# A chunked delta rule on one core: output transposes in four banks, projection in two, and squares, closing norm and output scaling at other slots

## The chip, the cores and the metric

The kernel runs on one core of a Trainium2 chip. The metric is the device time of one execution in microseconds (us). The engines are named as in the profile: PE is TensorE's matmuls and PEld its weight loads, DVE is VectorE, ACT is ScalarE, POOL is GpSimd, and SP (in the timeline SPq) issues most DMAs.

## The reference

The program is four layers over 16 sequences of 512 tokens of 256 channels: a gated linear attention, a mixture of experts, a gated delta rule, and a feed-forward with composed weights. The change touches only the third, whose reference is, cut to its core:

```python
h = _rmsnorm(_layernorm(x, ln1_g, ln1_b), rms_in_w)
q = _causal_conv_silu(h @ Wq, conv_q_w).reshape(b, t, H, Kd)      # H 4, Kd 64, Vd 128
k = _causal_conv_silu(h @ Wk, conv_k_w).reshape(b, t, H, Kd)
v = _causal_conv_silu(h @ Wv, conv_v_w).reshape(b, t, H, Vd)
q = _l2norm(q) * Kd ** (-0.5)
k = _l2norm(k)
g = -jnp.exp(A_log) * jax.nn.softplus(h @ Wa + dt_bias)
beta = jax.nn.sigmoid(h @ Wb)
...
def step(S, inp):
    q_t, k_t, v_t, g_t, b_t = inp
    S = S * jnp.exp(g_t)[..., None, None]
    delta = (v_t - jnp.einsum('bhk,bhkv->bhv', k_t, S)) * b_t[..., None]
    S = S + k_t[..., :, None] * delta[..., None, :]
    return (S, jnp.einsum('bhk,bhkv->bhv', q_t, S))
...
o = _rmsnorm(o, o_norm_w) * jax.nn.silu(h @ Wg)
x = x + o @ Wo
x_out = jax.nn.gelu(_layernorm(x, ln2_g, ln2_b) @ W2 + b2, approximate=False) + x
```

A plain layer norm over the channels follows each layer. The one after the delta rule is the closing norm here. All is float32.

## The kernel before

`delta_rule` takes one sequence a period. A sequence is four chunks of 128 tokens (`TT` = 4), worked in two pairs. The periods are a pipeline: in period b the recurrence of sequence b runs (`here`), while sequence b+1 is projected and convolved (`front`), b+2 is mixed from the experts and normed (`ln`), b-1 gets its last two chunks, its gate, its output projection and the dense layer (`past`), and b-2 its GELU and closing norm (`end`). There are periods -2 to 17. Periods 2 to 13 stand in a hardware loop, two to a turn; period 14 still has all but `ln`.

A period has 16 slots. Each engine has its own `period` function, which writes out the order of its work slot by slot. Nothing is scheduled at run time: each engine works through its queue in that order and waits on semaphores, one for each kind of result. So the order of the lines inside a slot is the order on the engine. A name in `wait("og", 1)` is the semaphore `s["og"]`, here "o is scaled".

For each pair the path is this. `key_products` (TensorE, slots 0 and 8) fills four banks with key by key and key by query products. `products` (VectorE) multiplies them by the decay into `nAT` and `QD`. `send_blocks` (SP) sends the 16 by 16 diagonal blocks of `nAT` to DRAM and reads them back block by block, `invert_blocks` (POOL) inverts them, and `return_blocks` (SP) puts them into `T`. Three levels double the inverted blocks (slots 5 to 7 for pair 0, 13 to 15 for pair 1). In each, `first_half` (TensorE) turns `T` into bank `UT` and multiplies `nAT` into a bank of `YZ`, `half_level` (ScalarE) copies both to `U` and `Y`, `second_half` (TensorE) multiplies them, and `merge` (VectorE) puts the result into `T`; the last level gives `Uf`. Bank `UT` is one for both chunks, so the second chunk's transposes wait for the first one's copy of `U`. The next key products wait for `Uf`.

`chunk` has three parts: `ks` and `R` (part 0), the deltas `dl` and their copy `de` (part 1), the state `S` and the output `o` (part 2). Its slots are in `CHUNK_AT`. Chunk 0 has slots 9 to 11, chunk 1 slots 12 to 14, chunks 2 and 3 slots 0 to 5 of the next period.

The outputs of sequence b-1 go this way: `squares` and `lengths_o`, the power -0.5 on POOL (`orr`), `gated` (the product with the gate), `unit_o` (16 scalings of 128 by 128 on ScalarE), `turn_o` (TensorE, 4 transposes for each of 4 column groups), `turned_o` (the copy to `y`), `mix_out` (the output projection in halves), `residual`, `norm3`, `turn_n`, `dense`. Before the change `turn_o`, `mix_out`, `turn_n`, `dense` and `gate` all use one bank, `SIDE`. `tap` is ScalarE's first term of the convolution, `conv` VectorE's other three, `conv_silu` the silu, `to_tokens` the turn back, `spread_out` its copy.

## Time and profile before

| what | value |
|---|---|
| median of 3 runs | 4717.77 us (4705.86 to 4723.58) |
| profiled execution, own time | 4709.05 us |
| its span | 4707.4 us |
| mean granted TensorE clock | 0.907 of 2.4 GHz |
| PE busy over the span | 4038.7 us (86%) |
| DVE, ACT, POOL busy | 2471.9, 1984.9, 1055.9 us |

The profile page gives the busy time of each engine over the whole program. The delta rule fills the part from about 2100 to 4236 us; what stands in it is read from the timeline, the waits and the table by stretches. A busy time says nothing about who waits for whom; an idle time in brackets in the timeline does, with the engine and line that ended it. The granted clock is 1.0 at 2.4 GHz and 0.5 at 1.2 GHz.

### The profile page before, as it was taken

The numbers are of one execution on the slowest core, as the hardware profiler recorded it, in microseconds if no ns is written. First come the engines' busy times: TensorE is split into PE (matmuls) and PEld (weight loads), VectorE is DVE, ScalarE is ACT, GpSimd is POOL, SyncE is SP. The second block draws the span as 40 slices with busy tenths as digits, with TensorE's granted clock in tenths as the row PEclk, the third lists the DMA queues.
The fourth block names the chain that finished last, engine by engine and source line by source line (L and its number), as shares of the span: only waits on it lengthen the run. The fifth ranks groups of instructions, "written<-read, shape, count | busy, mean of one in ns | idle before, by whom it ended". The sixth has DMA issues, their size and how long they took to land. (4 is left out here: it accounts for less than half of the span.)

```text
span 4707.4 us, 72598 instructions
## 1 busy us (share of the span) xinstructions
PE 4038.7 (86%) x23892; PEld 3132.2 (67%) x23892; DVE 2471.9 (53%) x5457; ACT 1984.9 (42%) x4069; POOL 1055.9 (22%) x1689
## 2 busy tenths in 40 slices
PE   5887887689999999966888888888888888859998
PEld 3555555368888888854666667666666666646666
DVE  7888887432222222225666676766666766421111
ACT  5656564112112211214565565555555555422222
POOL 0111111101221122123333333333333332200000
PEclk8888888899999999987899898888898988879999
DMA  1100100344555555541111111111111110011111
GB/s 33 37 32 27 41 28 28 102 139 171 179 181 189 185 179 181 190 131 52 37 37 37 42 37 41 41 41 32 40 33 37 41 40 21 22 37 58 58 57 46
DMA packets 220431, 345.98 MB, mean 73 GB/s; under 512 B 99956, under 2 KB 171380, under 8 KB 201972
## 3 DMA queue, kind: packets, MB, share of 16 engines
q1 hardware_dynamic: 196404, 271.69, 18.2%
q0 software_dynamic: 23760, 71.07, 4.8%
q8 instruction: 126, 2.06, 0.2%
q14 instruction: 141, 1.16, 0.1%
HBM read 275.56 MB, written 67.63 MB: 73 GB/s over the span
## 5 line engine op out<-in xcount | busy, mean ns | idle before, releaser
L539 ACT ACTIVATE moe_rel<-moe_fc 128x512 f32<-128x512 f32 x284 | 169.6, 597 | 798.7 <-PE moe_fc L504 798.7
L504 PE MATMUL moe_fc<-moe_xT,moe_win 128*128 128x256 f32 x2272 | 504.0, 380 | 1.5 <-issue 0.8
L515 PE MATMUL moe_o<-moe_wout,moe_hT 128*128 128x256 f32 x2272 | 502.0, 379 | 0.0
L504 PEld LDWEIGHTS moe_fc<-moe_xT,moe_win 128*128 128x128 f32 x2272 | 432.9, 191 | 61.2 <-issue 2.1
L515 PEld LDWEIGHTS moe_o<-moe_wout,moe_hT 128*128 128x128 f32 x2272 | 426.3, 190 | 55.1
L563 DVE TENSOR_TENSOR moe_hT<-moe_rel 128x512 f32<-128x512 f32 x284 | 196.6, 692 | 366.5 <-ACT moe_rel L539 366.5
L1781 DVE SCALAR_TENSOR_TENSOR gdr_y<-gdr_bank,gdr_cw,gdr_y 128x511 f32<-128x511 f32 (+2 forms) x384 | 287.5, 749 | 52.6 <-ACT gdr_y L2045 29.0
L2242 PE MATMUL gdr_bank<-gdr_hT,gdr_wqkv 128*128 128x512 f32 x512 | 282.5, 680 | 21.3 <-ACT gdr_qk L2060 15.8
L572 DVE COPY moe_osb<-moe_o 128x512 f32<-128x512 f32 x71 | 49.1, 692 | 424.9 <-PE moe_o L515 424.9
L2361 PE MATMUL gdr_bank<-gdr_ident,gdr_T 128*128 128x128 f32 x768 | 132.5, 301 | 126.5 <-DMA gdr_T<-blocks_in 76.0
L693 PE MATMUL ffn_fc<-ffn_xT,ffn_win 128*128 128x512 f32 x512 | 224.0, 596 | 2.0 <-DMA ffn_win<-ffn_w 2.0
L704 PE MATMUL ffn_o<-ffn_wout,ffn_hT 128*128 128x256 f32 x1024 | 225.2, 381 | 0.0
L737 DVE TENSOR_TENSOR ffn_z<-ffn_o,ffn_xres 128x512 f32<-128x512 f32 x32 | 20.6, 686 | 384.3 <-PE ffn_o L704 384.3
L2365 PE MATMUL gdr_bank<-gdr_T,gdr_nAT 128*128 128x64 f32 x1536 | 215.6, 289 | 0.0
L718 ACT ACTIVATE ffn_hT<-ffn_fc 128x512 f32<-128x512 f32 x128 | 76.4, 597 | 328.2 <-PE ffn_fc L693 328.2
L2361 PEld LDWEIGHTS gdr_bank<-gdr_ident,gdr_T 128*128 128x128 f32 x768 | 102.6, 157 | 166.8 <-issue 74.6
L704 PEld LDWEIGHTS ffn_o<-ffn_wout,ffn_hT 128*128 128x128 f32 x1024 | 193.2, 190 | 27.6
L2365 PEld LDWEIGHTS gdr_bank<-gdr_T,gdr_nAT 128*128 128x128 f32 x1536 | 211.6, 213 | 0.0
L1673 POOL TENSOR_TENSOR gdr_rstd<-gdr_var,gdr_mhalf 128x4 f32<-128x4 f32 x64 | 65.1, 1017 | 648.7 <-DVE gdr_var L91 500.7
L2142 ACT COPY gdr_U<-gdr_bank 128x512 f32<-128x512 f32 x192 | 112.4, 585 | 215.2 <-PE gdr_bank L2361 206.1
L2242 PEld LDWEIGHTS gdr_bank<-gdr_hT,gdr_wqkv 128*128 128x128 f32 x512 | 100.3, 212 | 138.3 <-issue 84.0
L693 PEld LDWEIGHTS ffn_fc<-ffn_xT,ffn_win 128*128 128x128 f32 x512 | 97.8, 191 | 118.9 <-issue 118.2
(394 smaller groups left out, 8591.8 us busy)
## 6 DMA issues: line engine op xcount, KB each, us to landing
moe_win<-in_moe_w SPq DMA_DIRECT2D x71, 1024.0 KB, 8.0
moe_wout<-in_moe_w SPq DMA_DIRECT2D x71, 1024.0 KB, 5.1
slots_out<-moe_osb POOLq DMA_DIRECT2D x71, 256.0 KB, 7.4
ffn_xin<-mixed_rows SPq DMA_DIRECT2D x17, 512.0 KB, 3.8
gla_xp<-in_xT_rows SPq DMA_DIRECT2D x16, 512.0 KB, 4.7
gla_xres<-in_x_rows SPq DMA_DIRECT2D x16, 512.0 KB, 3.9
token_rows<-gla_x POOLq DMA_DIRECT2D x16, 512.0 KB, 3.4
rt_W<-in_fc_b SPq DMA_DIRECT2D x32, 256.0 KB, 3.3
```

What stands on the lines that cost most here:

```text
L504: ins = nc.tensor.matmul(fc_ps[j][:, m % 2, :], win[u][:, c, m * P:(m + 1) * P], xT[:, c, :], start=(c == 0), stop=(c == DT - 1))
L515: ins = nc.tensor.matmul(o_ps[u][:, t, :], hT[u][:, k, t * P:(t + 1) * P], wout[u][:, k, :], start=(k == 0), stop=(k == FT - 1))
L539: nc.scalar.activation(rel[:, j, :, :], fc_ps[j][:], ACT.Relu).then_inc(relu_done, 1)
L563: nc.vector.tensor_tensor(hT[u][:, 2 * j:2 * j + 2, :], rel[:, j, :, :], rel[:, j, :, :], ALU.mult).then_inc(h_ready, 1)
L693: ins = nc.tensor.matmul(fc_ps[m % 4][:], win[:, c, m * P:(m + 1) * P], xT[:, c, :], start=(c == 0), stop=(c == DT - 1))
L704: ins = nc.tensor.matmul(o_ps[t // 2][:, t % 2, :], hT[:, k, t * P:(t + 1) * P], wout[:, k, :], start=(k == 0), stop=(k == FT - 1))
L718: nc.scalar.activation(hT[:, m, :], fc_ps[m % 4][:], ACT.Gelu_apprx_tanh).then_inc(h_ready, 1)
L1781: ins = stt(y[:, n % 4, d:L], bank[FRONT[n % 2]][:, 0:L - d], cw[:, n, 3 - d:4 - d], y[:, n % 4, d:L], ALU.mult, ALU.add)
L2142: done("U", n, copy(U[t][:], heads(bank[UT][:])))
L2242: ins = mm(bank[FRONT[n % 2]][:], wqkv[:, c, n * P:(n + 1) * P], hT[:, c, :], start=(c == 0), stop=(c == DT - 1))
L2361: ins = tp(bank[UT][:, h * P:(h + 1) * P], T[:, i, h, :], ident[:])
L2365: ins = mm(bank[YZ[i]][:, h * HP:(h + 1) * HP].rearrange("p (m n) -> p m n", n=half), nAT[:, i, h, :], first, start=True, stop=True)
```

## The change

`turn_o` writes each of its four column groups to a bank of its own (0, 1, 2, 3) and waits only for that group's scaling; `unit_o` scales one group at a call. `mix_out` uses bank 3 for its first half and bank 0 for its second, and both wait only for the four copies. `products` makes both chunks' `nAT` first, marked by a new semaphore `na` on which SP's send waits, and both `QD` after. The other lines are moves between slots: `squares(3)` and `squares_qk` from slot 5 to 6 on ScalarE, the closing norm's sum and scaling on VectorE from slots 9 and 10 to 2 and 4 and its power on POOL ahead of the others, the key lengths from slot 6 to 7, `unit_o` from slot 8 to 7 and 8, the four turned groups and copies to slot 9, the projection to 10 and 11, and rates, residuals and `norm2` around them. The diff, its lines cut to those that the text speaks of, indentation reduced:

```diff
+TURN_O, MIX = (UT, YZ[0], YZ[1], SIDE), (SIDE, UT)
...
     def send_blocks(pair, b):
-        sp.wait_ge(s["qd"], b * TT + 2 * pair + 2)
+        sp.wait_ge(s["na"], b * TT + 2 * pair + 2)
...
+        if end:
+            power(b - 2, var[1][:], rstd[1][:], "tl_var", 2, "tl_rstd", TT)
...
     def products(pair, b):
         wait, done = waiter(dve, b)
-        for t in (2 * pair, 2 * pair + 1):
-            i = t % 2
-            wait("kk", t + 1)
+        made = lambda i, k: bank[KKB[i][k]][:].rearrange("p (w n j) -> p w n j", w=2, n=H2)
+        for i in range(2):
+            wait("kk", 2 * pair + i + 1)
             for k in range(2):
-                made = bank[KKB[i][k]][:].rearrange("p (w n j) -> p w n j", w=2, n=H2)
-                stt(nAT[:, i, k::2, :], made[:, 0, :, :], -1.0, DT_[i][:, k::2, :], ALU.mult, ALU.mult)
-                ins = tt(QD[t][:, k::2, :], made[:, 1, :, :], DT_[i][:, k::2, :], ALU.mult)
+                ins = stt(nAT[:, i, k::2, :], made(i, k)[:, 0, :, :], -1.0, DT_[i][:, k::2, :], ALU.mult, ALU.mult)
+            done("na", 2 * pair + i + 1, ins)
+        for i in range(2):
+            t = 2 * pair + i
+            for k in range(2):
+                ins = tt(QD[t][:, k::2, :], made(i, k)[:, 1, :, :], DT_[i][:, k::2, :], ALU.mult)
             done("qd", t + 1, ins)
...
-            if slot == 6 and past:
-                lengths_o(b - 1)
...
+            if slot == 2 and end:
+                last_sum(b - 2)
             if slot == 3 and ln:
                 mix(0, b + 2)
             if slot == 4 and past:
                 gated(0, b - 1)
             if slot == 4 and ln:
                 mix(1, b + 2)
+            if slot == 4 and end:
+                last_norm(b - 2)
...
+                lengths_o(b - 1)
                 gated(1, b - 1)
-            if slot == 6 and front:
+            if slot == 7 and front:
                 lengths(b + 1)
-            if slot == 9 and end:
-                last_sum(b - 2)
-            if slot == 10 and end:
-                last_norm(b - 2)
             if slot == 9 and front:
+                rates(0, b + 1)
                 unit(b + 1)
             if slot == 10 and front:
-                rates(0, b + 1)
-            if slot == 10 and ln:
-                norm2(b + 2)
-            if slot == 11 and front:
                 rates(1, b + 1)
                 keys_beta(b + 1)
+            if slot == 10 and past:
+                residual(0, b - 1)
             if slot == 11 and past:
-                residual(0, b - 1)
-            if slot == 12 and past:
                 residual(1, b - 1)
-            if slot == 12 and ln:
-                rms(0, b + 2)
+            if slot == 11 and ln:
+                norm2(b + 2)
             if slot == 13 and past:
                 norm3(b - 1)
             if slot == 13 and front:
                 decay(b + 1, w)
                 values_beta(0, b + 1, w)
+            if slot == 13 and ln:
+                rms(0, b + 2)
...
-    def unit_o(b):
+    def unit_o(h, b):
         wait, done = waiter(act, b)
         act.wait_ge(gate_step, b * 2 + 2)
         wait("orr", 1)
-        for h in range(DH):
-            for t in range(TT):
-                part = o[:, t, h * VD:(h + 1) * VD]
-                ins = a_op(part, part, ACT.Copy, scale=orr[:, t * DH + h:t * DH + h + 1])
-        done("og", 1, ins)
+        for t in range(TT):
+            part = o[:, t, h * VD:(h + 1) * VD]
+            ins = a_op(part, part, ACT.Copy, scale=orr[:, t * DH + h:t * DH + h + 1])
+        done("og", h + 1, ins)
...
-            if past and slot in (10, 11):
-                turned_o(2 * slot - 19, b - 1)
...
+            if past and slot == 9:
+                turned_o(0, b - 1)
+                turned_o(1, b - 1)
             if front and 2 <= slot <= NP_ + 1:
                 spread_out(slot - 2, b + 1)
+            if past and slot == 9:
+                turned_o(2, b - 1)
+                turned_o(3, b - 1)
+            if past and slot == 8:
+                unit_o(2, b - 1)
+                unit_o(3, b - 1)
             if past and 1 <= slot <= TT:
                 gate(slot - 1, b - 1)
             if front and 1 <= slot <= NP_:
                 conv_silu(slot - 1, b + 1)
             if slot == 0 and end:
                 gelu(b - 2)
+            if past and slot == 6:
+                squares(3, b - 1)
+            if front and slot == 6:
+                squares_qk(b + 1)
+            if past and slot == 7:
+                unit_o(0, b - 1)
             if front and slot < NP_:
                 tap(slot, b + 1)
-            if past and slot in (9, 10):
-                turned_o(2 * slot - 18, b - 1)
-            if past and slot in (3, 5):
-                squares(2 if slot == 3 else 3, b - 1)
+            if past and slot == 7:
+                unit_o(1, b - 1)
+            if past and slot == 3:
+                squares(2, b - 1)
             if here and slot in (12, 15):
                 squares(0 if slot == 12 else 1, b)
-            if front and slot == 10:
+            if front and slot == 9:
                 rates(0, b + 1, w)
             if here and slot in (1, 2):
                 decay_keys(slot - 1, b)
-            if past and slot == 8:
-                unit_o(b - 1)
-            if here and slot in (9, 11):
-                decay_keys(2 if slot == 9 else 3, b)
-            if front and slot == 5:
-                squares_qk(b + 1)
-            if ln and slot == 11:
-                lengths_u(b + 2)
+            if here and slot == 11:
+                decay_keys(2, b)
+                decay_keys(3, b)
             if front and slot == 12:
                 rates(1, b + 1, w)
                 channels(0, b + 1, w)
             if front and slot == 13:
                 channels(1, b + 1, w)
                 keep_keys(b + 1)
+            if ln and slot == 12:
+                lengths_u(b + 2)
...
     def turn_o(c, b):
         wait, _ = waiter(pe, b)
-        wait("oTe", c) if c else wait("og", 1)
+        wait("og", c + 1)
         for t in range(TT):
-            ins = tp(bank[SIDE][:, tokens(t)], o[:, t, c * P:(c + 1) * P], ident[:])
+            ins = tp(bank[TURN_O[c]][:, tokens(t)], o[:, t, c * P:(c + 1) * P], ident[:])
         mark("oT", ins)
 
     def mix_out(p, b):
         wait, _ = waiter(pe, b)
-        wait("xe", 1) if p else wait("oTe", DH)
+        wait("oTe", DH)
         for t in (2 * p, 2 * p + 1):
             for c in range(DH):
-                ins = mm(bank[SIDE][:, (t % 2) * D:(t % 2 + 1) * D], y[:, c, tokens(t)], wo_s[:, c, :],
+                ins = mm(bank[MIX[p]][:, (t % 2) * D:(t % 2 + 1) * D], y[:, c, tokens(t)], wo_s[:, c, :],
                          start=(c == 0), stop=(c == DH - 1))
         mark("en", ins)
...
+            if past and slot == 10:
+                mix_out(0, b - 1)
             if here and lv >= BASE:
+                if slot == 13 and past:
+                    pe.wait_ge(s["xe"], b * 2)
                 first_half(lv, 2 * pair, b)
-            if past and slot in (10, 11):
-                turn_o(2 * slot - 19, b - 1)
...
+            if front and slot == 9:
+                rates(b + 1)
+            if past and slot == 9:
+                if here:
+                    pe.wait_ge(s["qd"], b * TT + TT)
+                turn_o(0, b - 1)
+                turn_o(1, b - 1)
             if front and 2 <= slot <= NP_ + 1:
                 to_tokens(slot - 2, b + 1)
             if here and lv >= BASE:
                 gate(slot - 1, b - 1)
             if front and slot < NP_:
                 project(slot, b + 1)
-            if front and slot == 9:
-                rates(b + 1)
-            if past and slot in (9, 10):
-                if slot == 9 and here:
-                    pe.wait_ge(s["qd"], b * TT + TT)
-                turn_o(2 * slot - 18, b - 1)
-            if past and slot in (11, 12):
-                mix_out(slot - 11, b - 1)
+            if past and slot == 9:
+                turn_o(2, b - 1)
+                turn_o(3, b - 1)
+            if past and slot == 11:
+                mix_out(1, b - 1)
```

How this moves ScalarE's queue around the squares, in slots 5 and 6 of a steady period (`gdr_bank0` is `UT`, `gdr_sq<-gdr_qk` the squares of q and k, `gdr_scr,gdr_ov<-gdr_o` those of o, `gdr_y<-gdr_bank` the taps). Before:

```order
L2045 ACTIVATE gdr_y<-gdr_bank7,gdr_cw 128x512
L2118 ACTIVATE gdr_scr,gdr_ov<-gdr_o 128x128 x4
L2093 ACTIVATE gdr_sq<-gdr_qk 128x2048
...
L2142 COPY gdr_U0<-gdr_bank0 128x512
L2144 COPY gdr_Y0<-gdr_bank1 128x256
...
L2142 COPY gdr_U1<-gdr_bank0 128x512
L2144 COPY gdr_Y1<-gdr_bank2 128x256
```

And in the changed kernel:

```order
L2047 ACTIVATE gdr_y<-gdr_bank7,gdr_cw 128x512
...
L2143 COPY gdr_U0<-gdr_bank0 128x512
L2145 COPY gdr_Y0<-gdr_bank1 128x256
...
L2143 COPY gdr_U1<-gdr_bank0 128x512
L2145 COPY gdr_Y1<-gdr_bank2 128x256
L2062 COPY gdr_vn<-gdr_bank6 128x4x128
L2052 ACTIVATE gdr_y<-gdr_y 128x512
L2119 ACTIVATE gdr_scr,gdr_ov<-gdr_o 128x128 x4
L2095 ACTIVATE gdr_sq<-gdr_qk 128x2048
...
L2047 ACTIVATE gdr_y<-gdr_bank6,gdr_cw 128x512
```

The two squares have moved from ahead of the four copies of `U` and `Y` to behind them, the spread and the silu, directly ahead of the tap of slot 6.

TensorE's queue in slots 9 to 12 (`gdr_ident,gdr_o` are the turned outputs, `gdr_wo,gdr_y` the output projection, `gdr_R,gdr_U0` to `QD0` chunk 0, `gdr_wab` the rates). Before:

```order
L2257 MATMUL gdr_bank6<-gdr_wab,gdr_hT 128x8 x8
L2386 MATMUL gdr_bank3<-gdr_ident,gdr_o 128x128 x8
L2306 MATMUL gdr_bank4<-gdr_R,gdr_U0 128x128 x4
L2386 MATMUL gdr_bank3<-gdr_ident,gdr_o 128x128 x8
L2313 MATMUL gdr_bank4<-gdr_dl,gdr_kd 64x128 x4
L2317 MATMUL gdr_bank5<-gdr_dl,gdr_QD0 128x128 x4
L2394 MATMUL gdr_bank3<-gdr_wo,gdr_y 128x256 x8
...
L2296 MATMUL gdr_bank4<-gdr_S,gdr_XT0 128x256 x2
L2300 MATMUL gdr_bank5<-gdr_S,gdr_XT0 128x256 x2
...
L2394 MATMUL gdr_bank3<-gdr_wo,gdr_y 128x256 x8
...
L2334 MATMUL gdr_bank7<-gdr_sp,gdr_upto 128x16
```

And in the changed kernel:

```order
L2268 MATMUL gdr_bank6<-gdr_wab,gdr_hT 128x8 x8
L2397 MATMUL gdr_bank0<-gdr_ident,gdr_o 128x128 x4
L2397 MATMUL gdr_bank1<-gdr_ident,gdr_o 128x128 x4
...
L2260 MATMUL gdr_bank7<-gdr_ident,gdr_y 128x128 x4
L2397 MATMUL gdr_bank2<-gdr_ident,gdr_o 128x128 x4
L2397 MATMUL gdr_bank3<-gdr_ident,gdr_o 128x128 x4
L2405 MATMUL gdr_bank3<-gdr_wo,gdr_y 128x256 x8
L2317 MATMUL gdr_bank4<-gdr_R,gdr_U0 128x128 x4
L2324 MATMUL gdr_bank4<-gdr_dl,gdr_kd 64x128 x4
L2328 MATMUL gdr_bank5<-gdr_dl,gdr_QD0 128x128 x4
L2405 MATMUL gdr_bank0<-gdr_wo,gdr_y 128x256 x8
...
L2307 MATMUL gdr_bank4<-gdr_S,gdr_XT0 128x256 x2
L2311 MATMUL gdr_bank5<-gdr_S,gdr_XT0 128x256 x2
...
L2345 MATMUL gdr_bank7<-gdr_sp,gdr_upto 128x16
```

The transposes of o stand together in banks 0 to 3 around the last turn of y (`gdr_ident,gdr_y`), the first half of the projection has moved ahead of chunk 0's deltas, and the second ahead of chunk 1.

## Rows read from the trace of the kernel before

**Rows 1.** Stretches: length; busy us of PE, PEld, DVE, ACT, POOL; PEclk; DMA

```profile
2364.00:4089.00 1725.00, 1469.46 (x9230) 1178.03 (x9227) 1153.69 (x2668) 1000.87 (x2401) 566.36 (x1075) 0.89 0.13 37
3119.50:3133.10 13.60, 9.08 (x43) 7.55 (x43) 10.89 (x27) 11.80 (x29) 10.22 (x22) 0.50 0.14 45
3218.50:3228.80 10.30, 10.30 (x40) 8.13 (x38) 4.70 (x7) 3.00 (x6) 0.00 (x0) 0.50 0.00 0
```

**Rows 2.** Timeline of POOL: start, duration in us, line, out<-in; one period

```profile
3103.40 5.43 POOL L1673 TENSOR_TENSOR gdr_ssq<-gdr_ssq,gdr_mhalf 128x32 f32<-128x32 f32 x1 [11.06 <-DVE gdr_ssq L1791]
...
3229.26 5.43 POOL L1673 TENSOR_TENSOR gdr_ssq<-gdr_ssq,gdr_mhalf 128x32 f32<-128x32 f32 x1 [10.85 <-DVE gdr_ssq L1791]
```

**Rows 3.** Waits of TensorE, 2700 to 4000 us: total us, times, longest

```profile
PE gdr_bank L2361 <- ACT gdr_U L2142: 38.0, 11, 3.5
PE gdr_bank L2361 <- DMA gdr_T<-blocks_in: 34.7, 11, 4.3
...
PE gdr_bank L2386 <- ACT gdr_y L2149: 20.8, 21, 1.2
```

**Rows 4.** Timeline of ScalarE, slot 5

```profile
3215.25 1.91 ACT L2093 ACTIVATE gdr_sq<-gdr_qk 128x2048 f32<-128x2048 f32 x1
```

**Rows 5.** Timeline of TensorE, slots 5 to 8; brackets: idle before, and releaser

```profile
3217.91 0.66 PE L2361 MATMUL gdr_bank<-gdr_ident,gdr_T 128*128 128x128 f32 x4 [3.44 <-ACT gdr_U L2142]
...
3224.04 3.73 PE L2242 MATMUL gdr_bank<-gdr_hT,gdr_wqkv 128*128 128x512 f32 x4
...
3234.15 1.98 PE L2242 MATMUL gdr_bank<-gdr_hT,gdr_wqkv 128*128 128x512 f32 x4
3236.06 0.50 PE L2346 MATMUL gdr_bank<-gdr_XT 64*128 64x128 f32 x4
```

**Rows 6.** Timeline of TensorE, slots 9 to 13 of the period before

```profile
3117.47 0.66 PE L2249 MATMUL gdr_bank<-gdr_ident,gdr_y 128*128 128x128 f32 x4 [3.01 <-ACT gdr_y L2050]
...
3122.52 1.09 PE L2386 MATMUL gdr_bank<-gdr_ident,gdr_o 128*128 128x128 f32 x4 [2.56 <-ACT gdr_o L2102]
...
3139.49 3.72 PE L2394 MATMUL gdr_bank<-gdr_wo,gdr_y 128*128 128x256 f32 x16 [0.88 <-DVE gdr_xa L1918]
...
3145.21 0.60 PE L2361 MATMUL gdr_bank<-gdr_ident,gdr_T 128*128 128x128 f32 x4
```

**Rows 7.** Timelines of SP, POOL, TensorE: the blocks' way, pair 1, pair 0

```profile
3114.27 3.63 SPq L1575 DMA_DIRECT2D blocks_out<-gdr_nAT  x8
...
3122.24 2.06 POOL L1679 TENSOR_TENSOR gdr_vblk<-gdr_wblk,gdr_low 64x256 f32<-64x256 f32 x1
...
3135.99 0.47 SPq L1582 DMA_DIRECT2D blocks_in<-gdr_vblk  x1
...
3177.51 3.63 SPq L1575 DMA_DIRECT2D blocks_out<-gdr_nAT  x8
...
3184.56 0.85 POOL L1679 TENSOR_TENSOR gdr_vblk<-gdr_wblk,gdr_low 64x256 f32<-64x256 f32 x1 [24.33 <-DMA gdr_wblk<-blocks_out]
...
3196.21 0.46 SPq L1582 DMA_DIRECT2D blocks_in<-gdr_vblk  x1
...
3203.19 0.66 PE L2361 MATMUL gdr_bank<-gdr_ident,gdr_T 128*128 128x128 f32 x4 [2.59 <-DMA gdr_T<-blocks_in]
```

**Rows 8.** Timeline of VectorE: key lengths, products, closing sum, R, S

```profile
3100.82 2.29 DVE L1790 TENSOR_REDUCE gdr_ssq<-gdr_sq 128x32 f32<-128x2048 f32 x1
...
3111.38 0.42 DVE L1861 SCALAR_TENSOR_TENSOR gdr_nAT<-gdr_bank,gdr_DT 128x256 f32<-128x256 f32 x1 [1.71 <-PE gdr_bank L2347]
...
3117.89 1.23 DVE L1940 TENSOR_TENSOR gdr_n<-gdr_x,gdr_xa 128x1024 f32<-128x1024 f32 x1
...
3121.09 0.17 DVE L1798 TENSOR_SCALAR gdr_ssq<-gdr_ssq 128x16 f32<-128x16 f32 x1
...
3190.79 1.13 DVE L1888 SCALAR_TENSOR_TENSOR gdr_R<-gdr_bank,gdr_gbn,gdr_v 128x128 f32<-128x128 f32 x4 [2.01 <-PE gdr_bank L2300]
...
3205.58 1.43 DVE L1894 SCALAR_TENSOR_TENSOR gdr_S<-gdr_S,gdr_gam,gdr_bank 64x128 f32<-64x128 f32 x4 [1.21 <-PE gdr_bank L2313]
```

14 lines of the change are left out of this document (6 added, 8 removed).

## The prediction

> **What bounds the kernel now.** I read the delta rule's stretch alone, since the change touches nothing else. First the table by stretches: from 2364 to 4089 us, where the periods are in their steady form, TensorE is busy 1469 of 1725 us at a mean granted clock of 0.89, VectorE 1154 and ScalarE 1001 [rows 1]. So TensorE is the engine to follow, and it loses time in two ways: it waits, and it runs at the lower of its two clock levels (1.2 instead of 2.4 GHz). Next one period: the same POOL power of the key lengths starts at 3103.40 and at 3229.26, so a period takes 125.86 us [rows 2]. Then the waits of TensorE [rows 3]: in 1300 us the copy of U costs 38.0 us in 11 waits (once a period, 3.5), the return of the inverted blocks 34.7 in 11, and the copies of turned outputs 20.8 in 21. In one period I see these and two more at their places [rows 5, 6]. The long ones are followed by half clock: in that period the granted clock is 0.50 for 13.6 us and for 10.3 us [rows 1], and these stretches begin 2.0 and 0.6 us after a wait of 3.01 and one of 3.44 us ended.
>
> Around them lies a chain that no idle engine shows. After the products of a pair, its 64 diagonal blocks travel: SP sends them (3177.51), POOL inverts them (3184.56), SP returns them (3196.21), TensorE's first level starts on them (3203.19) [rows 7]. From send to level that is 25.7 us, twice a period, and it is the floor under half a period: 25.7 us, then three levels, then the next key products, which wait for the last level.
>
> **The change part by part.** I name the two key products K0 (slot 0) and K1 (slot 8); the period is K0 to K1 to K0.
>
> *Squares (slots 5 to 6).* ScalarE now does the squares of o3 and of q and k ahead of the copy of U; the latter alone takes 1.91 us from 3215.25 [rows 4], and the transposes for the second chunk stand 3.44 us until that copy [rows 5]. Moved behind both half levels, they lie in front of one tap, where the projection that the tap needs ends only at 3224.04 + 3.73 [rows 5]. The wait goes: 3.4 us. With it goes its follower: the clock is 0.50 from 3218.5 to 3228.8, TensorE busy throughout [rows 1]; the same four projection passes take 3.73 us there and 1.98 later [rows 5], so 10.3 us shrink to 10.3 x 1.98 / 3.73 = 5.5, a gain of 4.8. Bounds of this part: 3.4 if the clock stays low, 8.2 if not. What is late next: following the queues with the durations of the trace, ScalarE reaches the tap of slot 6 some 1.5 us after its projection is done (the squares now lie there), VectorE's convolution and scans follow it, and the scans plus the last copies of U end about 6.5 us earlier than now. I take 6.5.
>
> *Key lengths (2.3 us, 3100.82 [rows 8]) from slot 6 to 7.* They leave the place ahead of the convolution and land ahead of products(1), where VectorE now waits 1.71 us for the key products [rows 8]. Cost 2.3 - 1.7 = 0.6 us while that wait is there; followed, with K1 early, products(1) start 2.5 us after K1 instead of 1.2, so 1.3.
>
> *Products split.* The blocks' send waits for four multiplications instead of eight. One is 0.42 us long [rows 8], so the send leaves 1.3 to 1.6 us earlier, twice a period. For pair 0 the wait is 2.59 us [rows 7], about half of it goes; but VectorE has more to do there (next part). For pair 1 the key lengths take it back: 1.4 - 1.3 = 0.1.
>
> *Closing norm.* The last sum, 3.2 us from 3117.89 to 3121.09 [rows 8], and its scaling (estimate 1.2 us: the sum alone took 1.23 for as many elements) leave slots 9 and 10 for slots 2 and 4. VectorE has waits there of 2.01 us before R and 1.21 before S [rows 8]; the 4.4 us fill these and leave about 0.7 us of lateness at the merges of slot 5, hidden by the blocks' wait as long as it is above that. Net of this and the earlier send in the first half: 0 to -1 us, I take -0.5. On POOL the power of that norm no longer stands between 3121 and 3122.24 in front of the second inversion, which started only then although the blocks had been sent at 3114.27 [rows 7]; pair 0 needed 7.05 us for that way, so pair 1 gains 3122.24 - 3121.3 = 0.9 us.
>
> *Outputs (slots 7 to 12).* The 16 scalings of o are cut into four groups, two of them before the last tap and restart, in slot 7; the four turned groups go to four banks, so none waits for the copy of the one before; the projection has two, so its second half no longer waits for the residual. Waits that this takes: 2.56 us on the scaling and 0.88 on the residual [rows 6], and the copies' 1.2 us at most each, two a period [rows 3]. The 3.01 us before the last turn of y [rows 6] are filled by the rates and two of the turned groups. Together about 8 us off TensorE's queue. New waits: all four copies must end before the first mix_out (about 2.6 us, by hand), and S of chunk 0 now stands on VectorE behind the second rates, kb and the residual: by hand, it comes about as long after K1 as now. TensorE could start the first level of pair 1 some 29 us after K1 instead of 35.0 (3145.21 less 3110.2, one period before 3236.06 [rows 5, 6]). But the blocks can't be there sooner than products(1) + 25.7: 2.5 (above) + 1.4 for four multiplications + 25.7 = 29.6 us after K1. If POOL takes the 13.75 us that it took for pair 1 (3122.24 to 3135.99) and not the 11.65 of pair 0 [rows 7], 31.7. So this part gives 3.3 to 5.4; I take 3.7, since ScalarE's queue is full there and I took each crossing between engines for nearly free.
>
> *xe wait, extra bank guards, more semaphores:* long fulfilled when reached; 0.
>
> Steady period: 6.5 + 0.5 + 3.7 = 10.7; less some 0.7 for crossings, 10.0 us. There are 13 such periods (2 to 14). Period 1 lacks only the closing norm: 8. Period 0 has two waits for blocks and the squares: 5. Period 15 has no front and waits for blocks twice: 3. The tail: 1. Sum 130 + 17 = 147 us. The profiled execution took 4709.05 us, within the three runs (median 4717.77), so 4717.8 - 147 = 4571; I say 4575.
>
> A row to weigh: turned groups of 128 columns run 1.09 us for four at 3122.52 [rows 6] inside the half-clock stretch. If that stretch stays, nothing is lost in my sum, because the blocks' arrival ends the half.
> On this the Trainium skill ("TensorE: Matmul & The Clock Gate", "A second HAM failure mode: psum-queue depth-cycling") warns that cycling a matmul's outputs through banks leaves many short idle gaps, so that the clock swings; that speaks against four banks. By that rule the sum would lose what the clock gives in part one: it is the rival B below.
>
> **The rivals.**
> *A, forecast (0.50):* both gaps close; 4575, own range 4540 to 4610.
> *B, the clock stays low (0.17).* TensorE still idles in pieces, and the half-clock stretches move instead of going. Speaks for it: 23.9 us per period at 0.5 now, after waits of only 3.0 and 3.4 us; against: these very pieces go. Then part one gives 3.4 instead of 6.5 and the second half about 2.7: 6 a period, 78 + 12 = 90 us, 4628.
> *C, the next queue binds (0.22).* VectorE and ScalarE are fuller where I put the moved work, and 1154 of 1725 us of VectorE are already in chains. The blocks' way gets no shorter than 25.7 us. If the filled slots 2 to 5 and the wait for S cost what the outputs gain, only the squares' wait and part of its clock are left: 4 a period, 60 us, 4658.
> *D, no measurable change (0.06):* the U wait is replaced by the tap's wait (the squares ahead of it, conv, scan and Uf behind), the rest as C: about 1 a period, 4703.
> *E, slower (0.05):* one mechanism: VectorE's queue order in slots 10 and 11. S of chunk 0 stands behind rates(1), which wait for ScalarE's exp, which waits for four copies, these for the scaling. If ScalarE gets there more than 11 us later than I reckon, chunk 1, the channels and the level come later than 35 us after K1; at 13 us late each period costs 2 us more: +30, 4748. The rows give ScalarE's queue there some 2 us of spread, hence the small chance.
>
> **How the numbers follow.** A measurement of this kernel tells 0.5% (24 us) from nothing. A, B and C are faster than 4694: 0.89; D 0.06 same; E 0.05 slower. Eight in ten takes A whole, B and C with their spread: 4530 (12.5 a period, all bounds at the good end) to 4680.
>
> **What would show it.** Right: the wait of L2361's transposes (the new L2372) for the copy of U gone; no half clock in slots 6 and 7; key products to key products about 56 us for K0 to K1 and 58 to 59 for K1 to K0; TensorE's wait on the returned blocks before the second pair new or grown, which is where the outputs' gain ends. Wrong: periods above 120 us, a new wait of TensorE for S (its state) or for the copies of turned outputs above 3 us, or half-clock time per period still near 24 us. The forecast fails most likely at the second half, where four engines' queues and the blocks' trip end within 2 us of each other.

## The result, and the profile after

The changed kernel takes 4592.78 us (median of 4 runs, 4580.92 to 4605.31) beside 4711.82 us for the kernel before (4 runs): ratio 0.9747, 95% interval 0.9717 to 0.9777, so 119 us faster. The forecast was 4575. Of the runs in the experiments, four executions took 5222.70 to 8034.73 us where the others of the same kernel agree within 1%; the ratios leave them out.

First the stretch 2364 to 4089 us (columns as in [rows 1]), and two pieces of the second half of one period:

```profile
2364.00:4089.00 1725.00, 1498.71 (x9632) 1202.85 (x9632) 1184.91 (x2778) 1040.99 (x2499) 603.22 (x1110) 0.92 0.14 38
...
3537.00:3541.00 4.00, 2.82 (x12) 2.42 (x12) 3.63 (x8) 3.84 (x9) 0.56 (x1) 0.57 0.36 108
...
3557.00:3564.50 7.50, 6.49 (x30) 5.82 (x31) 2.17 (x5) 4.56 (x15) 0.00 (x0) 0.54 0.05 6
```

The granted clock rose from 0.89 to 0.92, but pieces near 0.5 are left in the second half. The waits of TensorE, 2700 to 4000 us, answer to [rows 3]:

```profile
PE gdr_bank L2317 <- DVE gdr_R L1892: 25.1, 11, 3.8
PE gdr_bank L2288 <- ACT gdr_gam L2075: 24.7, 11, 2.2
PE gdr_bank L2260 <- ACT gdr_y L2052: 23.8, 21, 2.1
PE gdr_bank L2405 <- ACT gdr_y L2150: 22.9, 12, 3.0
PE gdr_bank L2372 <- DMA gdr_T<-blocks_in: 20.6, 8, 9.5
...
PE gdr_bank L2372 <- DVE gdr_T L1880: 9.0, 5, 2.2
...
PE gdr_bank L2372 <- ACT gdr_U L2143: 3.4, 12, 0.5
```

The wait for the copy of U fell from 38.0 to 3.4 us. New are one for the decay factors gam before the second third of the channels (24.7) and one for merged T (9.0). The one for the last copy of turned outputs before the projection has grown from 6.3 to 22.9, and the longest in total is now that for R, 25.1 where it was 16.9.

The timeline of TensorE shows K0 of period 1 and K0 of period 14, with 13 periods between them, and inside that stretch one whole second half, from K1 at 3528.03 to the K0 behind it at 3589.43:

```profile
2299.81 0.50 PE L2357 MATMUL gdr_bank<-gdr_XT 64*128 64x128 f32 x4
...
3528.03 0.50 PE L2357 MATMUL gdr_bank<-gdr_XT 64*128 64x128 f32 x4
...
3537.43 1.11 PE L2260 MATMUL gdr_bank<-gdr_ident,gdr_y 128*128 128x128 f32 x4 [2.08 <-ACT gdr_y L2052]
...
3541.70 3.72 PE L2405 MATMUL gdr_bank<-gdr_wo,gdr_y 128*128 128x256 f32 x16 [1.44 <-ACT gdr_y L2150]
...
3557.14 0.72 PE L2288 MATMUL gdr_bank<-gdr_ident,gdr_qk 128*128 128x128 f32 x4 [2.25 <-ACT gdr_gam L2075]
...
3559.82 1.12 PE L2372 MATMUL gdr_bank<-gdr_ident,gdr_T 128*128 128x128 f32 x4 [0.88 <-DMA gdr_T<-blocks_in]
3560.73 1.81 PE L2376 MATMUL gdr_bank<-gdr_T,gdr_nAT 128*128 128x64 f32 x8
3562.33 2.02 PE L2317 MATMUL gdr_bank<-gdr_R,gdr_U 128*128 128x128 f32 x8
...
3589.43 0.50 PE L2357 MATMUL gdr_bank<-gdr_XT 64*128 64x128 f32 x4
...
3822.92 0.50 PE L2357 MATMUL gdr_bank<-gdr_XT 64*128 64x128 f32 x4
```

A period is (3822.92 - 2299.81) / 13 = 117.2 us. The same two K0s of the kernel before stand at

```profile
2302.36 0.50 PE L2346 MATMUL gdr_bank<-gdr_XT 64*128 64x128 f32 x4
...
3919.00 0.50 PE L2346 MATMUL gdr_bank<-gdr_XT 64*128 64x128 f32 x4
```

which makes 124.4: 7.2 us a period and not 10.0. That is 94 of the 115 us by which the spans of the two traces differ (4707.4 and 4592.1); the other 22 lie ahead of this stretch (3) and behind it (19), where the forecast had some 17.

Split at the key products, as means over those 13 periods (us; "level" is the time from the key products to the first transpose of T after them; "half" is the time at the lower clock level, half clock from here on, read from the clock's records). The kernels below the second line are those of the experiments:

| kernel | K0 to K1 | level | half | K1 to K0 | level | half | period |
|---|---|---|---|---|---|---|---|
| before | 63.2 | 30.6 | 13.7 | 61.1 | 34.7 | 12.3 | 124.4 |
| changed | 56.2 | 30.3 | 3.9 | 61.0 | 32.4 | 12.3 | 117.2 |
| squares alone | 55.1 | 30.5 | 3.9 | 62.7 | 36.1 | 15.2 | 117.8 |
| products alone | 60.4 | 28.8 | 11.0 | 61.6 | 35.0 | 13.4 | 121.9 |
| norm alone | 62.9 | 30.9 | 11.3 | 60.9 | 34.4 | 12.1 | 123.7 |
| outputs alone | 62.5 | 30.3 | 12.9 | 62.7 | 33.2 | 13.1 | 125.3 |
| squares and products | 52.8 | 28.9 | 1.0 | 62.9 | 36.4 | 15.2 | 115.7 |
| changed, squares undone | 63.2 | 30.3 | 13.9 | 59.3 | 30.7 | 8.1 | 122.5 |

The first half gained the 7.0 us that were forecast (63 to 56). The second should have gained 3.7 and gained 0.2: the level starts 2.3 us earlier, but from there to K0 it now takes 28.6 us and not 26.5. Of the 12.3 us of half clock 3.9 now stand behind the level, where the kernel before has none. The products of T and nAT behind the level run at half clock in the period shown: for 1.81 us at 3560.73 the same form at full clock needs

```profile
3564.73 1.00 PE L2376 MATMUL gdr_bank<-gdr_T,gdr_nAT 128*128 128x64 f32 x8
```

The way of the blocks in that half starts with VectorE's products and SP's send:

```profile
3531.08 1.54 DVE L1861 SCALAR_TENSOR_TENSOR gdr_nAT<-gdr_bank,gdr_DT 128x256 f32<-128x256 f32 x4
```
```profile
3532.66 4.49 SPq L1576 DMA_DIRECT2D blocks_out<-gdr_nAT  x8
```

Products(1) begin 3.05 us after K1, the send leaves at K1 + 4.6, and 27.2 us later the level starts. Here it waits 0.88 us for the blocks, but that holds for only 3 of the 13 periods. In the other ten the blocks are there (they land at K1 + 31.4 on average), and TensorE's own queue reaches the level later, as in the period before (K1 at 3413.07), after the same wait for gam:

```profile
3444.54 0.76 PE L2288 MATMUL gdr_bank<-gdr_ident,gdr_qk 128*128 128x128 f32 x4 [2.25 <-ACT gdr_gam L2075]
...
3446.14 1.06 PE L2372 MATMUL gdr_bank<-gdr_ident,gdr_T 128*128 128x128 f32 x4
```

### The profile page after: what moved, and what is told of

It reads as the page before. It is cut to its first block and busy times, and to the rows that moved or that the text cites. A ratio compares the mean times of both kernels' runs of the same rounds, so it can differ in the third digit from the quotient of the medians.

```text
span 4592.1 us, 72682 instructions
## 1 busy us (share of the span) xinstructions
PE 3992.8 (87%) x23892; PEld 3096.7 (67%) x23892; DVE 2463.9 (54%) x5457; ACT 1991.3 (43%) x4069; POOL 1078.2 (23%) x1689
## 5 line engine op out<-in xcount | busy, mean ns | idle before, releaser
L504 PEld LDWEIGHTS moe_fc<-moe_xT,moe_win 128*128 128x128 f32 x2272 | 432.7, 191 | 61.2 <-issue 2.1
L515 PEld LDWEIGHTS moe_o<-moe_wout,moe_hT 128*128 128x128 f32 x2272 | 426.3, 190 | 55.1
L2253 PE MATMUL gdr_bank<-gdr_hT,gdr_wqkv 128*128 128x512 f32 x512 | 265.1, 643 | 29.9 <-ACT gdr_qk L2062 24.7
L460 POOL COPY moe_ix<-slot_token 128x2 uint32 (+1 forms) x71 | 12.5, 177 | 674.1 <-DMA slots_out<-moe_osb 475.4
```

The source lines that it names most:

```text
L504: ins = nc.tensor.matmul(fc_ps[j][:, m % 2, :], win[u][:, c, m * P:(m + 1) * P], xT[:, c, :], start=(c == 0), stop=(c == DT - 1))
L515: ins = nc.tensor.matmul(o_ps[u][:, t, :], hT[u][:, k, t * P:(t + 1) * P], wout[u][:, k, :], start=(k == 0), stop=(k == FT - 1))
L2253: ins = mm(bank[FRONT[n % 2]][:], wqkv[:, c, n * P:(n + 1) * P], hT[:, c, :], start=(c == 0), stop=(c == DT - 1))
```

## The experiments

The theory after the comparison: the squares carry nearly all of the gain, and the second half gives back on half clock what its waits lose. The rival is the forecast's own sum, in which the outputs part pays 3.7 us.

**The parts alone.** Four kernels, each the kernel before with one part.

*Squares.*
```diff
+                        if past and slot == 6:
+                            squares(3, b - 1)
+                        if front and slot == 6:
+                            squares_qk(b + 1)
...
-                        if slot == 6 and front:
+                        if slot == 7 and front:
                             lengths(b + 1)
```


> The kernel before with the squares part alone: squares of o3 and of q and k behind both half levels in slot 6, the output lengths behind them, the key lengths in slot 7. Theory 1 (the squares carry nearly the whole gain, 119 us): the wait of the second chunk's transposes for the copy of U goes, K0 to K1 falls from about 63 to about 57 us, K1 to K0 stays near 61, and the time falls by 80 to 110 us, to 4605 to 4635. The prediction's own term is the wait of 3.4 us and 10.3 us of half clock that shrink to 5.5, less 1.3 for the key lengths: 5 to 6.5 us in each of 13 periods and some 5 in the others, 70 to 90 us. Rival (the half clock stays when the queue is not emptied of its other waits): 3.4 us less 1.3 in a period, about 30 us, to 4680.

Measured: 4618.94, ratio 0.9810 (0.9793 to 0.9826): 91 us. K0 to K1 fell by 8.1 us; K1 to K0 grew by 1.5, as the key lengths put the level at K1 + 36.1. The rival is out: half clock in the first half fell from 13.7 to 3.9 us with the wait. But the 8.1 us are not the squares' alone, since the same part takes the key lengths (2.3 us of VectorE) out of slot 6; what that is worth shows further down.

*Products.*
```diff
-                    sp.wait_ge(s["qd"], b * TT + 2 * pair + 2)
+                    sp.wait_ge(s["na"], b * TT + 2 * pair + 2)
```
(and the loop over the four nAT ahead of that over the four QD)

> The kernel before with the products split alone (four multiplications, then the send of the blocks, then the other four). The prediction: the send leaves 1.3 to 1.6 us earlier twice a period; in the first half the wait on the blocks (2.59 us) shrinks by that, in the second half the level is not waited for by the blocks before, so 1.3 us in a period, about 18 us: 4694. Theory 1: the same. Rival (the wait is replaced by one for VectorE, which lies in its own chain): nothing, 4712.

Measured: 4673.77, ratio 0.9916 (0.9899 to 0.9932): 37 us by the medians, twice what was expected. The wait on the blocks fell from 34.7 us [rows 3] to

```profile
PE gdr_bank L2364 <- DMA gdr_T<-blocks_in: 11.8, 11, 1.8
```

that is by 2.1 us a period; the level comes 1.8 us earlier, and half clock in that half fell by 2.6 us.

*Closing norm.*
```diff
+                        if slot == 2 and end:
+                            last_sum(b - 2)
...
+                        if slot == 4 and end:
+                            last_norm(b - 2)
...
-                        if slot == 9 and end:
-                            last_sum(b - 2)
-                        if slot == 10 and end:
-                            last_norm(b - 2)
```


> The kernel before with the closing norm alone moved from slots 9 and 10 to slots 2 and 4 and its POOL power ahead of the first of the block inversions' followers. The prediction has 0.9 us for POOL in the second half and up to 1 us of lateness in the first, 0 to -1 us net: 4700 to 4712. Theory 1: the same, no difference that can be measured. Rival (the 4.4 us of VectorE in slots 2 and 4 make the merges late, TensorE waits for T in slot 5 and then runs at half clock, as in 3161 to 3175 of the changed kernel): slower by 2 to 4 us in a period, 4735 to 4765.

Measured: 4731.17, ratio 1.0039 (1.0025 to 1.0053), in 9 runs from 4705.88 to 4741.92: neither the equal time that was expected nor the rival's 4735 to 4765. The profiled execution is the fastest of the nine and its period is 0.7 us shorter than before, so the trace doesn't show where the others lost some 20 us.

*Outputs.*
```diff
-                    wait("oTe", c) if c else wait("og", 1)
+                    wait("og", c + 1)
...
-                        ins = tp(bank[SIDE][:, tokens(t)], o[:, t, c * P:(c + 1) * P], ident[:])
+                        ins = tp(bank[TURN_O[c]][:, tokens(t)], o[:, t, c * P:(c + 1) * P], ident[:])
```
(and all else of the diff but the other three parts)

> The kernel before with the outputs part alone (scalings in four groups, four banks for the turned outputs, two for the projection, rates, residual and the rest moved with them); squares, lengths, closing norm and products as before. The prediction's term is 3.7 us in a period, 50 us in all: 4660, with K1 to K0 at 57.5 us. Theory 1 (the half gives back on half clock what its waits lose): 0 to 1 us in a period, 4698 to 4718, K1 to K0 at 60 to 61.5. Rival (the part costs by itself, ScalarE's queue full): over 4725.

Measured: 4730.35, ratio 1.0048 (1.0032 to 1.0065): slower, by some 20 us, above both the forecast's term and the theory's range, and where the rival (the part costs by itself) had it. The level of the second pair now waits for its blocks too (21 waits where there were 11), and the new waits for the copies and for gam are there:

```profile
PE gdr_bank L2368 <- DMA gdr_T<-blocks_in: 55.9, 21, 4.1
...
PE gdr_bank L2401 <- ACT gdr_y L2148: 25.4, 10, 2.7
PE gdr_bank L2284 <- ACT gdr_gam L2073: 22.4, 10, 2.2
```

The level is 1.4 us earlier than before and K0 3.0 us later after it, with 6.1 us of half clock behind the level where the kernel before has none. So here the level's wait for its blocks, 2.1 to 3.5 us in every one of the 13 periods, stands ahead of the half clock.

**The changed kernel with something undone or added.** These four ran together at a time when the kernel before took 4793.77 us and not 4710 to 4717. The changed kernel itself did not run beside them, so their ratios can't be set against 0.9747; their traces are read half by half.

*Without the outputs part.*
```diff
-                            ins = mm(bank[MIX[p]][:, (t % 2) * D:(t % 2 + 1) * D], y[:, c, tokens(t)], wo_s[:, c, :],
+                            ins = mm(bank[SIDE][:, (t % 2) * D:(t % 2 + 1) * D], y[:, c, tokens(t)], wo_s[:, c, :],
```
(and all of that part)

> The changed kernel without the outputs part: the kernel before with squares, closing norm and split products. The single parts gave 91 us (squares), 37 (products), and the norm and the outputs cost some 20 each. If these add, this kernel is 108 to 128 us faster than before, about 4585 to 4600, and the outputs part is worth nothing or less. Rival, the prediction's own: the outputs give 3.7 us in a period once the squares' wait is gone, so this kernel is some 50 us slower than the changed one, about 4640.

Measured: 4690.65, ratio 0.9797 (0.9776 to 0.9819). Inconclusive: its second half is 68.8 us long, and in most periods holds this wait of TensorE for a copy of ScalarE. ScalarE itself stands still around it (the standstill, from here on), released by something that the trace only calls remote:

```profile
3532.50 1.94 PE L2381 MATMUL gdr_bank<-gdr_Y,gdr_U 128*128 128x64 f32 x8 [4.41 <-ACT gdr_Y L2146]
```
```profile
3525.52 0.37 ACT L2146 COPY gdr_Y<-gdr_bank 128x256 f32<-128x256 f32 x1 [0.98 <-remote]
3528.49 0.78 ACT L2156 ACTIVATE gdr_h2T<-gdr_bank,gdr_bb,gdr_g 128x512 f32<-128x512 f32 x1 [2.60 <-issue]
3531.36 0.59 ACT L2144 COPY gdr_U<-gdr_bank 128x512 f32<-128x512 f32 x1 [2.10 <-remote]
```

No kernel outside these four has a wait of ScalarE or VectorE of over 0.9 us with that releaser in the 13 periods. Here it falls some 50 us after K1, on the path; in the three kernels below some 58 to 64 us after K1, just ahead of K0. It doesn't fall in the first half, which gives 54.7 us for K0 to K1 here; but where it stands just ahead of K0, the first R of the first half can come late by it (6.0 to 6.5 us after K0 in many of the even periods, mostly 4.7 in the changed kernel).

*Key lengths back in slot 6.*
```diff
-                        if slot == 7 and front:
+                        if slot == 6 and front:
                             lengths(b + 1)
```


> The changed kernel with the key lengths back in slot 6, ahead of the convolution and not ahead of products(1). Theory (the 2.29 us ahead of products(1) delay the send of the blocks and with them the second half): the first level of pair 1 comes 1 to 1.5 us earlier, K1 to K0 falls from 60.5 to 59.5, and the time falls by 10 to 20 us, to about 4575 to 4583. Rival (VectorE's convolution at slot 6 sets the pace of the queue, as the prediction let the lengths leave it): K0 to K1 grows by as much, 4590 to 4600.

Measured: 4612.49, ratio 0.9615 (0.9590 to 0.9640). The level is at K1 + 31.0, but K0 to K1 is 58.3 us, with a wait that the changed kernel all but lacks (0.2 us in total):

```profile
PE gdr_bank L2357 <- DVE gdr_U L1875: 19.7, 11, 2.0
```

The rival holds: in slot 6 the lengths delay the convolution, the scans and the last copies of U, for which K1 waits. So the lengths' place is worth 2.1 us of the first half (58.3 and 56.2), or 2.4 beside the fillers (55.9), and that is in the 8.1 us of squares alone.

*Closing norm back in slots 9 and 10* (the closing norm's diff above, reversed).

> The changed kernel with the closing norm back in slots 9 and 10. Theory (moving it out gives the second half 0.9 us on POOL and its 4.4 us of VectorE, and costs the first half up to 1): within 0.5% of the changed kernel, 4585 to 4605. Rival 1 (the norm in slots 2 and 4 makes the merges late and now and then puts a long stretch of half clock there, as in the one period of 125 us): faster, 4570 to 4585. Rival 2 (the second half of the changed kernel lives on the room that the norm left): slower by over 1 us in a period, above 4610.

Measured: 4631.18, ratio 0.9668 (0.9645 to 0.9691). K0 to K1 is 53.7 us, where the changed kernel has 56.2 and the fillers, which ran beside it, 55.9; its K1 to K0, 65.2, holds the standstill. So in slots 2 and 4 the norm costs the first half 2.2 to 2.5 us; what it is worth in the whole can't be read. The kernel without outputs, which has the norm there but not the outputs part, is at 54.7, 1.9 above squares and products (52.8, below).

*Fillers.*
```diff
+                def fill_reads(t, b, u):
+                    wait, _ = waiter(pe, b)
+                    wait("qse", t + 1)
+                    for _ in range(4):
+                        for n in range(H2):
+                            mm(bank[CHUNK[1]][:, 2 * n * VD:2 * (n + 1) * VD], ident[:], flat(S[:, n, :, :]), start=True, stop=True)
```


> The changed kernel with matmuls that compute nothing, in TensorE's idle pieces of the second half: 16 transposes of o behind the first two turned groups, 8 products of the identity with S (256 columns each) ahead of the first output projection, and 8 ahead of the channels that wait for gx. Each filler is 2.1 us long at the full clock and stands where 1.4 to 2.3 us of waiting are. Theory (short idle pieces bring the half clock, and this costs the second half what its waits no longer cost): the half-clock time in K1 to K0 falls from 13.4 us to under 8 and the half by 1 to 3 us, 4550 to 4580. Rival (the half clock doesn't hang on these pieces, or the blocks' trip sets the end of the half anyway): the time of the changed kernel or up to 15 us more, 4590 to 4608.

Measured: 4602.03, ratio 0.9610 (0.9591 to 0.9628). The two fillers of products take 16 matmuls each and not 8, so together they are

```profile
3542.33 1.91 PE L2405 MATMUL gdr_bank<-gdr_ident,gdr_o 128*128 128x128 f32 x16
3545.94 3.62 PE L2412 MATMUL gdr_bank<-gdr_S,gdr_ident 128*128 128x256 f32 x16
3562.94 3.72 PE L2412 MATMUL gdr_bank<-gdr_S,gdr_ident 128*128 128x256 f32 x16 [0.46 <-ACT gdr_QSe L2128]
```

9.3 us of work that computes nothing. One whole period half and the steady stretch:

```profile
3535.00:3598.00 63.00, 57.10 (x424) 51.62 (x425) 40.75 (x97) 35.85 (x94) 25.56 (x45) 1.00 0.14 39
```
```profile
2700.00:4000.00 1300.00, 1177.62 (x7993) 952.70 (x7993) 917.17 (x2126) 807.48 (x1931) 461.43 (x842) 0.99 0.14 38
```

Half clock in K1 to K0 is 0.3 us, and that half takes 61.2 us with 9.3 us more work in it; the changed kernel took 61.0 in its own run, with 12.3 us of half clock. Waits of TensorE there are 3.9 us and not 7.9. So of the 9.3 us some 4.0 are filled waits, and the other 5.3 should be what the full clock gave back. The first part of the theory is borne out (the idle pieces bring the half clock), the second (1 to 3 us shorter) is not. These fillers were as long as what they saved; and the rival's second reason, that the blocks' trip sets the end, holds in part: the level waits for its blocks in 8 of the 13 periods, where the changed kernel does in 3. Behind the level the half still takes 28.2 us and not 26.5, now with 0.3 us of half clock and 2.0 us of idle time. But the standstill falls into that stretch, so this doesn't settle what full clock alone would give back there.

**The changed kernel again, with three others beside it.** These four ran together, and the kernel before took 4717.14 us. They bear the same chip number as the four above, which were measured 17 minutes earlier.

> The changed kernel itself, as the measure for the others of this call, since the kernel before took 4710 us on one chip and 4794 on another. If the ratio holds from chip to chip: 0.972 to 0.978. Rival (a chip on which more of the kernel before runs at half clock gains more from the change): 0.960 to 0.967, beside which the changed kernel with one part undone (0.9615 with the lengths, 0.9668 with the norm, 0.9797 without the outputs) must be read.

Measured: 4595.17, ratio 0.9738 (0.9704 to 0.9771), the same as the first time.

*Squares and products alone* (the two parts above, together).

> The kernel before with the squares part and the split products, without the outputs part and with the closing norm in its old place. If the single parts add up (squares 0.981, products 0.9916, outputs and norm 1.0048 and 1.0039), this is faster than the whole change: 0.973, with the whole change at 0.975 or more. Rival (the outputs part pays only where the squares are gone: with it the second half is a queue short of TensorE's waits): slower than the whole change by 1.5 to 4 us in a period, 0.5 to 1.2% above it.

Measured: 4592.60, ratio 0.9747 (0.9724 to 0.9770): the same as the whole change, and neither faster nor slower as the two expectations had it. So outputs and norm together are worth nothing that can be measured. Its timeline beside that of the changed kernel shows what the first half of that one pays. In the changed kernel, from K0 at 3357.9:

```profile
3373.89 1.22 DVE L1944 TENSOR_TENSOR gdr_n<-gdr_x,gdr_xa 128x1024 f32<-128x1024 f32 x1
...
3377.47 1.13 DVE L1892 SCALAR_TENSOR_TENSOR gdr_R<-gdr_bank,gdr_gbn,gdr_v 128x128 f32<-128x128 f32 x4 [0.29 <-issue]
...
3390.88 1.38 DVE L97 TENSOR_SCALAR gdr_x<-gdr_n,gdr_agg,gdr_rstd 128x256 f32<-128x256 f32 x4
...
3397.05 0.44 DVE L1880 COPY_PREDICATED gdr_T<-gdr_level,gdr_bank 128x256 f32<-128x256 int32 x1
...
3397.55 0.66 PE L2372 MATMUL gdr_bank<-gdr_ident,gdr_T 128*128 128x128 f32 x4 [2.18 <-DVE gdr_T L1880]
```

And in this one, from K0 at 3339.8:

```profile
3358.14 1.13 DVE L1891 SCALAR_TENSOR_TENSOR gdr_R<-gdr_bank,gdr_gbn,gdr_v 128x128 f32<-128x128 f32 x4 [2.02 <-PE gdr_bank L2304]
...
3376.38 0.44 DVE L1879 COPY_PREDICATED gdr_T<-gdr_level,gdr_bank 128x256 f32<-128x256 int32 x1
...
3376.88 0.66 PE L2365 MATMUL gdr_bank<-gdr_ident,gdr_T 128*128 128x128 f32 x4 [0.20 <-DVE gdr_T L1879]
```

R comes 19.6 us after K0 and not 18.3, the merges 39.2 and not 36.6, and over the 13 periods the merges are later by the same 2.6 us: the closing norm stands ahead of both. The wait for T of about 2.2 us comes in six of the 13 periods. In the longest first half of the changed kernel (64.9 us, from K0 at 3117.6) it is followed by half clock for 14 us:

```profile
3161.43 0.94 PE L2372 MATMUL gdr_bank<-gdr_ident,gdr_T 128*128 128x128 f32 x4 [2.24 <-DVE gdr_T L1880]
```
```profile
3161.00:3175.00 14.00, 13.57 (x54) 11.40 (x55) 7.77 (x21) 8.20 (x19) 3.99 (x2) 0.52 0.11 38
```

*Fillers with the lengths in slot 6.*

> The changed kernel with both the matmuls that compute nothing in the second half and the key lengths in slot 6. With the lengths in slot 6 the first level of pair 1 came at K1 + 31.0 and not + 33.0 on the same chip as the fillers, and with the fillers the half had no half clock. If both effects are real and stand side by side: 10 to 25 us below the changed kernel. Rival (the convolution is later by the lengths, K0 to K1 58.3 and not 55.9, and takes the gain): the time of the fillers alone, 0.961 on that chip.

Measured: 4627.01, ratio 0.9807 (0.9779 to 0.9835), 0.7% slower than the changed kernel beside it, and not 10 to 25 us faster. The rival holds: K0 to K1 is 57.8 us, with the wait for the last copies of U again, and once the fillers hold the queue full the first transposes of a level wait for a copy of U that stands on ScalarE behind squares(0):

```profile
PE gdr_bank L2359 <- DVE gdr_U L1875: 20.2, 11, 2.0
PE gdr_bank L2374 <- ACT gdr_U L2143: 16.5, 21, 1.5
```

The fillers' effect is there without the standstill too: half clock in K1 to K0 is 4.5 us, and TensorE is busy for 1550.21 of 1725 us at 0.97, with the half 61.5 us long:

```profile
2364.00:4089.00 1725.00, 1550.21 (x10335) 1265.52 (x10335) 1185.05 (x2773) 1040.06 (x2491) 592.91 (x1108) 0.97 0.14 37
```

*Squares undone.*
```diff
-                        if past and slot == 3:
-                            squares(2, b - 1)
+                        if past and slot in (3, 5):
+                            squares(2 if slot == 3 else 3, b - 1)
+                        if front and slot == 5:
+                            squares_qk(b + 1)
```


> The changed kernel with squares, output lengths and key lengths back where they were before. The theory that the squares carry the gain: 85 to 110 us slower than the changed kernel, a ratio to before of 0.993 to 1.000, K0 to K1 back at 60 to 63 us with the wait for the copy of U at 3.4. Rival (the other parts together give as much once they all stand): 50 us slower or less, a ratio of 0.985 or under.

Measured: 4667.52, ratio 0.9900 (0.9881 to 0.9920), 73 us slower than the changed kernel: between the expectation (85 to 110) and its rival (50 or less). K0 to K1 is back at 63.2 us with the wait:

```profile
PE gdr_bank L2371 <- ACT gdr_U L2144: 36.5, 13, 3.5
```

Its second half, though, is the shortest of all, 59.3 us with the level at K1 + 30.7 and 8.1 us of half clock: here the outputs part, with the split products and the norm moved out, does pay, 1.9 us against before. The lengths in slot 6 should make the difference to the changed kernel's 61.0: with them there the level was at K1 + 31.0 above too. K0 to K1 also splits the 7.0 us: from 63.2 here to 58.3 with the lengths still in slot 6 is 4.9 for the squares, and from there to 56.2 is 2.1 for the lengths, as far as runs of different times can be compared.

## Why the prediction was right, and where a term was off

- *The squares, 6.5 us.* Right in mechanism; the part measured 8.1. The wait went (38.0 to 3.4) and its half clock with it. That equals the upper bound of 8.2, but partly by luck. The bound was worked out for the wait and its clock alone, from a period with 10.3 us of half clock, where the mean is 13.7; and with the lengths still in slot 6 the squares gave only 4.9. The key lengths' leaving the place ahead of the convolution gave some 2.1, for which the sum has no term of its own.
- *Key lengths, 1.3 us at products(1).* Right: K1 to K0 grew by 1.5 in squares alone.
- *Products split, 1.3 us in the first half, 0.1 in the second.* Too small: 2.8 in the first half when alone and 2.3 beside the squares (55.1 to 52.8). The forecast counted the earlier send but not the half clock that follows the wait it shortens (13.7 to 11.0 us). In the second half it gave nothing (61.1 to 61.6), near the 0.1 forecast.
- *Closing norm, the first half net -0.5.* The net came out: from squares alone (55.1) to squares, products and norm (54.7, the kernel without outputs) is 0.5. Its terms did not. What failed is "leave about 0.7 us of lateness at the merges of slot 5, hidden by the blocks' wait". The merges come 2.6 us later, TensorE waits 2.2 us for T in six of the 13 periods, and half clock in that half is 3.9 and not 1.0 us. Its covers were the blocks' wait and the wait for U, and the same change shortens the one and takes away the other. The norm costs 1.9 to 2.5 us.
- *Outputs, put at nothing in the first half.* From squares and products to the whole change K0 to K1 grows by 3.4 us. With the norm at 1.9 to 2.5, the outputs part holds the other 0.9 to 1.5. By which wait, no run shows.
- *First half in all.* 6.5 + 0.5 = 7.0 was forecast and 7.0 came, but as 8.1 + 2.3 - 3.4. That the sum met is luck.
- *Outputs, 3.7 us in the second half.* This is the term that made the forecast's gain too large, 147 us where 119 came. Three of its steps failed.
  - TensorE was to reach the level 29 us after K1, with about 8 us of waits off its queue and 2.6 new; its waits ahead of the level fell only from 8.4 to 6.8 us a period, since gam (2.25), the last y (1.9), the copies (1.8) and dl (0.8) remain or are new. The wait for gam had no term. So the level came at K1 + 32.4, 2.3 us earlier than before.
  - The blocks were to come at 29.6 to 31.7 and land at 31.4 on average, since products(1) began at 3.05 and not 2.5 and the trip took 27 us; they set the level in 3 of 13 periods, so the wait on them is only in part where the gain ends.
  - The sum took everything behind the level as unchanged, while the waits for gam (2.25) and for the blocks (0.88) are followed by a granted clock of 0.54 for 7.5 us in the period shown: 3.9 us of half clock stand behind the level on average, and 2.1 us go back there. That the half clock is what costs these 2.1 us is an estimate from the clock's records (3.9 us at half clock can cost 2.0); with the fillers it was gone and that stretch stayed at 28.2 us, but with the standstill in it.

  The copies' wait stood at 3.0 at most, at the bound that was given for it.
- *Rivals.* B (the clock stays low) was wrong for the first half and right for the second, where half clock stayed at 12.3 us. C (VectorE's fuller slots 2 to 5 cost what the outputs gain) is what happened to norm and outputs; its total was too high, since squares and products gave more than it had. D and E didn't come: no wait for S among the longest.

The Trainium skill ("TensorE: Matmul & The Clock Gate", "A second HAM failure mode: psum-queue depth-cycling") tells of a kernel in which cycling through PSUM banks left frequent small idle gaps and the clock swung; that spoke against four banks. The outputs part, which has the banks in it, raised the half clock of the second half by 0.8 us (12.3 to 13.1, outputs alone), but moved it: 6.1 of it stand behind the level, where there was none. That small idle gaps bring the swings, the trace and the fillers bear out.

Left open: what the norm in its old place is worth in the whole change, since that kernel ran only beside the standstill; the squares moved with the key lengths left in slot 6 and nothing else changed; fillers just as long as the idle pieces; whether the stretch behind the level would be back at 26.5 us with full clock and no standstill; and why the norm alone was slower in eight of nine executions than in the ninth. No version measured here beats the changed kernel; squares and products do as well with two small edits.

## What to carry to other kernels

Price a wait of TensorE with the half clock that follows it: here the wait of 3.5 us, gone together with the key lengths' 2.3 us ahead of the convolution, was worth 8.1, and 2.1 us less of the blocks' wait were worth 2.8. And when several edits share one path, ask of each hidden cost whether its cover is one of the waits that another edit removes: the norm's 4.4 us on VectorE would have been free only as long as other waits stood behind them. Ask too which queue reaches the next step last: where two end within 1 us of each other, as TensorE's and the blocks' do here, shortening one of them shows little. Undo or do each part alone before keeping it; two of the four parts here carry the whole gain.

## What was not expected of the hardware

- 9.3 us of empty matmuls per period, put into idle pieces of 1.4 to 2.3 us, left the half as long as it was, with the granted clock at 1.00 in it and 0.99 over 1300 us (0.92 before them).
- The kernel before took 4793.77 us at one time and 4710 to 4717 at others, the last of them 17 minutes later under the same chip number, so the runs don't show that it is a matter of the chip. In the four kernels that ran beside the 4793.77, ScalarE and VectorE stood still once a period for 2 to 5 us, at a place that differed between kernels. What stops them the trace doesn't say.
